# A layer kernel on one core: full-height content matmuls, PSUM tiles emptied by two engines, and a content copy moved behind the exponentials

## The reference

```
xn = layernorm(x)
c_q = xn @ Wq_down          # latent 64
c_kv = xn @ Wkv_down        # latent 64
q_c = c_q @ Wq_up;  k_c = c_kv @ Wk_up;  v_c = c_kv @ Wv_up      # 128 heads x 4
q_r = xn @ Wq_rope          # 128 heads x 64
k_r = xn @ Wk_rope          # 64, shared by all heads
scores = (q_c . k_c + q_r . k_r) / sqrt(68)
s = (softmax(scores) @ v_c) @ Wo
g = silu(ffn(xn))
out = x + s * g
```

## Time and profile before

| | |
|---|---|
| median of the runs | 2092.19 us |
| the profiled execution's own time | 2091.22 us |
| its span | 2089.4 us |
| TensorE busy | 2027.3 us (97%) |
| VectorE, ScalarE, GpSimd busy | 1396.4, 1068.5, 496.7 us |
| preamble, up to the first matmul of attention | 104.36 us |

### The profile page before, as it was taken

The page is one execution under the profiler, slowest core; times in us unless marked ns, Lnnn a source line. Parts: engine busy times, 40 slices in busy tenths (PEclk is TensorE's granted clock), DMA queues, the critical chain, the costliest instruction groups (busy, mean ns, idle before and its releaser), DMA issues. The chain is left out here.

```text
span 2089.4 us, 38976 instructions
## 1 busy us (share of the span) xinstructions
PE 2027.3 (97%) x12576; PEld 1542.7 (74%) x12576; DVE 1396.4 (67%) x1606; ACT 1068.5 (51%) x1549; POOL 496.7 (24%) x771
## 2 busy tenths in 40 slices
PE   6989999999999999999999999999999999978998
PEld 4567777777777777777777777777777777746776
DVE  5376676666766676667666766676667666736764
ACT  3635555555555555555555555555555555542222
POOL 2122222222213232223132212231322222133221
PEclk7989999999999999999999999999999999999999
DMA  5511212121212121212121111111111111131221
GB/s 181 189 32 34 44 29 47 27 48 28 47 28 48 25 46 27 48 28 47 28 45 30 41 32 40 36 37 38 38 36 36 37 37 30 26 110 64 88 85 45
DMA packets 128841, 102.70 MB, mean 49 GB/s; under 512 B 51494, under 2 KB 94502, under 8 KB 128798
## 3 DMA queue, kind: packets, MB, share of 16 engines
q1 hardware_dynamic: 128798, 102.15, 20.9%
HBM read 50.71 MB, written 25.17 MB: 36 GB/s over the span
## 5 line engine op out<-in xcount | busy, mean ns | idle before, releaser
L707 DVE TENSOR_REDUCE mx<-sx 128x4 f32<-128x1024 f32 x512 | 627.1, 1225 | 501.3 <-PE sx L789 483.1
L687 ACT ACTIVATE probs<-st 128x1024 f32<-128x1024 f32 x512 | 512.0, 1025 | 150.3 <-PE st L772 148.7
L657 ACT ACTIVATE slot<-pj 64x512 fp32r<-64x512 f32 x512 | 303.9, 594 | 485.2 <-PE pj L802 478.9
L606 POOL CAST k<-kc 64x512 fp32r<-64x512 f32 x256 | 167.3, 654 | 1199.0 <-PE st L772 1198.7
L772 PE MATMUL st<-slot,k 89*128 89x512 f32 x1024 | 423.7, 414 | 10.3 <-ACT probs L687 2.8
L802 PE MATMUL pj<-xh,wh 128*128 128x512 f32 x1024 | 402.7, 393 | 4.6 <-PEq L154 3.6
L772 PE MATMUL st<-slot,krlh 128*128 128x512 f32 x1024 | 406.8, 397 | 0.0
L802 PE MATMUL pj<-xh,wl 128*128 128x512 f32 x1024 | 402.1, 393 | 0.0
L802 PE MATMUL pj<-xl,wh 128*128 128x512 f32 x1024 | 401.8, 392 | 0.0
L717 DVE TENSOR_TENSOR slot<-pj,slot 64x512 fp32r<-64x512 f32 x512 | 352.7, 689 | 16.3 <-ACT slot L657 0.3
L789 PEld LDWEIGHTS sx<-k,slot 88*128 88x128 f32 x2048 | 307.0, 190 | 65.6 <-issue 27.2
(11 more groups left out here) (172 smaller groups left out, 1406.4 us busy)
## 6 DMA issues: line engine op xcount, KB each, us to landing
w_stage<-in_Wq_rope SPq DMA_DIRECT2D x64, 256.0 KB, 3.1
c_scratch<-stage SPq DMA_DIRECT2D x32, 256.0 KB, 2.5
c_in<-c_scratch SPq DMA_DIRECT2D x128, 64.0 KB, 1.9
o_scratch<-o_sb SPq DMA_DIRECT2D x128, 64.0 KB, 2.2
k<-kc SPq DMA_DIRECT2D x128, 48.0 KB
slot<-kc SPq DMA_DIRECT2D x256, 24.0 KB
k<-kx SPq DMA_DIRECT2D x128, 48.0 KB
slot<-kx SPq DMA_DIRECT2D x256, 24.0 KB
```

What stands on the lines that cost most here:

```text
L606: nc.gpsimd.tensor_copy(k1[0:64, s, :, :].rearrange("p a n -> p (a n)"), krh[:, bp * CH:(bp + 1) * CH]).then_inc(k_ready, 1)
L657: nc.scalar.activation(slot1[0:64, (k - 1) % NS, e, :, :], pj[64 * e:64 * e + 64, :].rearrange("p (a n) -> p a n", a=2), ACT.Copy).then_in ...
L687: nc.scalar.activation(probs[:, k % NS, kt], st[:, kt], ACT.Exp, scale=SCALE).then_inc(exp_done, 1)
L707: nc.vector.tensor_reduce(mx[:, p, lo:lo + 4], sx[:, :, :].rearrange("p a (b k) -> p (a b) k", b=2), axis=AX.X, op=ALU.max).then_inc(red_d ...
```

## The change

It has five parts.

1. The low-part content matmuls (L413, L417, L421) take all 128 rows of `upl` and `cs` and not 64 of them. They then also add low x low, which is tiny.
2. Of the 12 content tiles of chunks 0 to 2, ScalarE empties ten and VectorE two (n = 3 and 8); of chunk 3, every second one goes to VectorE. One semaphore for each engine's tiles takes the place of the common one.
3. On VectorE `normalise` of the next chunk comes after the two remainders of `cs`, and not ahead of them behind the statistics. The remainders `xl` are spread between its tiles, and the statistics of the chunk after next stand at the end.
4. `project` multiplies by `wsh` first and by `wsl` last, and only the `wsl` matmuls wait for GpSimd. GpSimd's `wsl` waits for the first chunk's `xn`. Transposes stand ahead of odd tiles. The first content block `kc` is made behind chunk 1 and not at the end.
5. In attention `content_hi` comes behind the three exponentials of its step.

The diff, cut to its core:

```diff
+        def by_vector(u):
+            return u % NE % 2 == 1 if u // NE == NC - 1 else u % NE in (3, 8)
+        def wait_tile(eng, u):
+            done = sum(by_vector(v) == by_vector(u) for v in range(u + 1))
+            eng.wait_ge(dve_tiles if by_vector(u) else act_tiles, done)
...
             pool.wait_ge(ws_hi, 1)
+            pool.wait_ge(xn_ready, NTL)
             nc.gpsimd.tensor_tensor(wsl[:, :, :], ws[:, :, :], wsh[:, :, :], ALU.subtract).then_inc(ws_ready, 1)
...
                 for n in range(NE):
-                    if n % 2 == 0 and n < 2 * NTL and c + 1 < NC:
+                    u = c * NE + n
+                    if n % 2 == 1 and n < 2 * NTL and c + 1 < NC:
                         hi_transposed(c + 1, n // 2)
-                    u = c * NE + n
-                    act.wait_ge(ev_done, u + 1)
-                    if u >= NST:
-                        act.wait_ge(stored[u % NST], 16 * (u // NST))
-                    nc.scalar.activation(stage[:, u % NST, :], ev[n % 4][:, :], ACT.Copy).then_inc(st_ready, 1)
+                    if not by_vector(u):
+                        act.wait_ge(ev_done, u + 1)
+                        if u >= NST:
+                            act.wait_ge(stored[u % NST], 16 * (u // NST))
+                        nc.scalar.activation(stage[:, u % NST, :], ev[n % 4][:, :], ACT.Copy).then_inc(act_tiles, 1)
...
                 if c + 2 < NC:
                     root(c + 2)
-            act.wait_ge(c_loaded, 32)
-            nc.scalar.activation(kc[64:128, 0:CH], c_in[64:128, :], ACT.Copy).then_inc(ct_hi, 1)
+                if c == 1:
+                    act.wait_ge(c_loaded, 32)
+                    nc.scalar.activation(kc[64:128, 0:CH], c_in[64:128, :], ACT.Copy).then_inc(ct_hi, 1)
...
                 nc.vector.tensor_tensor(cs[0:64, 1, :], cp[64:128, :], cs[64:128, 1, :], ALU.subtract).then_inc(c_lo, 1)
+                if c + 1 < NC:
+                    normalise(c + 1)
                 dve.wait_ge(krh_done, 2 * c + 2)
                 nc.vector.tensor_tensor(krlh[0:64, xs], kp[0:64, :], krh[:, xs], ALU.subtract).then_inc(krl_done, 1)
-                if c + 1 < NC:
-                    for i in range(NTL):
-                        lo_transposed(c + 1, i)
+                for n in range(NE):
+                    u = c * NE + n
+                    if n % 2 == 1 and n < 2 * NTL and c + 1 < NC:
+                        lo_transposed(c + 1, n // 2)
+                    if by_vector(u):
+                        dve.wait_ge(ev_done, u + 1)
+                        if u >= NST:
+                            dve.wait_ge(stored[u % NST], 16 * (u // NST))
+                        nc.vector.tensor_copy(stage[:, u % NST, :], ev[n % 4][:, :]).then_inc(dve_tiles, 1)
                 if c + 2 < NC:
                     statistics(c + 2)
-                    normalise(c + 2)
...
                 for k in range(KD):
-                    for n, (w, xx) in enumerate(((wsh, xh), (wsh, xl), (wsl, xh))):
...
+                    for n, xx in enumerate((xh, xl)):
+                        nc.tensor.matmul(dst[:, :], wsh[:, k, lo:lo + 128], xx[:, k, xs],
+                                         start=(k == 0 and n == 0), stop=False)
+                pe.wait_ge(ws_ready, 1)
+                for k in range(KD):
+                    last = nc.tensor.matmul(dst[:, :], wsl[:, k, lo:lo + 128], xh[:, k, xs],
+                                            start=False, stop=(k == KD - 1))
...
-                    nc.tensor.matmul(ev[n % 4][:, :], upl[0:64, 0, i], cs[0:64, 0, :],
+                    nc.tensor.matmul(ev[n % 4][:, :], upl[:, a, i], cs[:, a, :],
                                      start=False, stop=True).then_inc(ev_done, 1)
...
-                if s == 2 and k < STEPS and at.live(k + 2):
-                    content_hi(k // NS + 1, at.turn(k) + 1)
...
                 if k % 2 == 0 and at.live(k - 3) and k - 3 < STEPS:
                     exponentials(at, k - 3, 0)
+                if s == 2 and k < STEPS and at.live(k + 2):
+                    content_hi(k // NS + 1, at.turn(k) + 1)
```

More of the change, by code:

```diff
@@ L195, in project_inputs @@
         ev_done = sem("ev_done")
-        st_ready = sem("st_ready")
+        act_tiles = sem("act_tiles")
+        dve_tiles = sem("dve_tiles")
+        def by_vector(u):
[3 more added lines that the diff above has]
+            eng.wait_ge(dve_tiles if by_vector(u) else act_tiles, done)
         def by_launch(t, a, j):
@@ L225, in _ @@
                 for n in range(NE):
-                    sp.wait_ge(st_ready, c * NE + n + 1)
+                    wait_tile(sp, c * NE + n)
                     i = n % NTL
@@ L382, in _ @@
             statistics(1)
-            normalise(1)
             for c in range(NC):
                 chunk(c)
-            dve.wait_ge(ct_hi, 1)
-            nc.vector.tensor_tensor(kc[64:128, 2 * CH:3 * CH], c_in[64:128, :], kc[64:128, 0:CH],
-                                    ALU.subtract).then_inc(ct_lo, 1)
+                if c == 1:
+                    dve.wait_ge(ct_hi, 1)
+                    nc.vector.tensor_tensor(kc[64:128, 2 * CH:3 * CH], c_in[64:128, :], kc[64:128, 0:CH],
+                                            ALU.subtract).then_inc(ct_lo, 1)
         @block.tensor
@@ L400, in project @@
             def project(c, dst, lo, done):
+                xs = slice(c * CH, (c + 1) * CH)
                 for k in range(KD):
-                    for n, (w, xx) in enumerate(((wsh, xh), (wsh, xl), (wsl, xh))):
-                        last = nc.tensor.matmul(dst[:, :], w[:, k, lo:lo + 128], xx[:, k, c * CH:(c + 1) * CH],
-                                                start=(k == 0 and n == 0), stop=(k == KD - 1 and n == 2))
+                    for n, xx in enumerate((xh, xl)):
[5 more added lines that the diff above has]
+                                            start=False, stop=(k == KD - 1))
                 last.then_inc(done, 1)
@@ L409, in raise_up @@
                 u = c * NE + n
-                wait(pe, st_ready, u - 3)
-                if a == 0:
-                    nc.tensor.matmul(ev[n % 4][:, :], uph[:, 0, i], cs[:, 0, :], start=True, stop=False)
-                    nc.tensor.matmul(ev[n % 4][:, :], upl[0:64, 0, i], cs[0:64, 0, :],
[L414 to L417, removed]
+                if u >= 4:
+                    wait_tile(pe, u - 4)
+                if a < 2:
+                    nc.tensor.matmul(ev[n % 4][:, :], uph[:, a, i], cs[:, a, :], start=True, stop=False)
+                    nc.tensor.matmul(ev[n % 4][:, :], upl[:, a, i], cs[:, a, :],
                                      start=False, stop=True).then_inc(ev_done, 1)
@@ L420, in raise_up @@
                     nc.tensor.matmul(ev[n % 4][:, :], cs[:, 1, i], uph[:, 2, :], start=True, stop=False)
-                    nc.tensor.matmul(ev[n % 4][:, :], cs[64:128, 1, i], upl[64:128, 2, :],
+                    nc.tensor.matmul(ev[n % 4][:, :], cs[:, 1, i], upl[:, 2, :],
                                      start=False, stop=True).then_inc(ev_done, 1)
@@ L428, in _ @@
                 pe.wait_ge(xl_done, (c + 1) * NTL)
-                if c == 0:
-                    pe.wait_ge(ws_ready, 1)
+                pe.wait_ge(ws_hi, 1)
                 wait(pe, c_lo, 2 * c)
```

## The result

The changed kernel takes 2041.03 us (median of four runs, 2040.73 to 2042.02) against 2092.16 us: a ratio of 0.9756, 95% interval 0.9739 to 0.9773. The forecast was 2043.7 us. The profiled execution took 2042.02 us with a span of 2040.2, so 49.2 us of span are gone. By milestones: attention starts at 76.53 and not at 104.36 us (27.8 us), attention itself is 22.2 us shorter (from its first matmul to the last group of `ob`, 1742.2 before and 1720.0 after), and what follows is 0.8 us longer.

The account below looks back on a forecast made before the run. TensorE, busy for 97% of the span, bounds it, slowed by weight-load stalls, low clock and waits. 2091.22 less 26.8 (preamble) and 21.7 (attention) gives 2042.7; the median lies 1.0 above, so 2043.7, range 2035 to 2058.

Parts of the forecast that it names:

- content behind the exponentials: Attention: 62 steps go from 6.94 to 6.59 us with the content copy after the third exponential, 21.7 us.
- Start: Chunk 0's start: wsl waits for normalise, so the first projection starts at 15.1 and not 16.9; bounds 0 to 2.1 us.
- The hold: Before the first content stage: content begins at 23.3, 5.1 us earlier, and idle time and low clock nearly go.
- Content stages: Chunks 0 to 2: chunk 0 takes 10.0 us; later chunks 14.2, of which content 8.6, with ScalarE late.
- the step that I had priced at 0 to 0.5: VectorE's statistics and ScalarE's root before the next cs, with kc in chunk 1: hidden, 0.5 us if not.
- The stall: Content pairs: 0.24 us idle ahead of 64-row weight loads goes with 128 rows; two matmuls then 0.23 us apart.
- Rival 1: Preamble: 64 rows cost nothing, content stays at 11.8 us a chunk; gain 15.6 and not 26.8, 2055; chance 0.06.
- Rival 2: Clock stays low in chunk 0 as TensorE waits: 5 us, 2049; through the whole preamble 2073; chance 0.09.
- Chunk 3: Last content stage: six stage buffers and stores at 0.84 us each hold it; twelfth tile written by 76.7.
- End of the preamble: Last tile to attention: kc made earlier, leaving 0.35 of DMA issue and 0.5; attention starts at 77.6.
- Rival 3: Attention: exponentials' own wait takes over, moving the copy gives little; half the gain 2055, none 2065; chance 0.10.
- Rival 4: Attention: GpSimd's copies hold VectorE's content remainder past its 0.9 us to spare; 2087 to 2130; chance 0.03.

Follow-up runs that it names:

- e4: Changed kernel with VectorE's normalise of the next chunk back behind the statistics, ahead of the remainders of cs; 2050.52 us.
- e6: Changed kernel with ScalarE emptying all content tiles, none left to VectorE; 2040.57 us.
- e2: Kernel before with one edit, low-part content matmuls on 128 rows; 2072.73 us.
- e1: Changed kernel with the low-part content matmuls on 64 rows again; 2054.20 us.
- e5: Kernel before, low parts still on 64 rows, content tiles taken two at a time (high, high, low, low); 2081.04 us.
- e10: Changed kernel with eight stage buffers and not six; 2041.23 us.
- e7: Changed kernel with the first content block made at the end of the preamble again; 2040.40 us.
- e11: Kernel before with attention's content copy behind the exponentials and nothing else; 2070.34 us.
- e3: Changed kernel with attention's content copy ahead of the exponentials again; 2065.40 us.

## Why the prediction was right, step by step

The direction, the time (2.7 us off) and both halves of the sum held: 26.8 forecast and 27.8 measured for the preamble, 21.7 and 22.2 for attention (0.8 more behind it). The three large terms (no stall between rows, no hold, content behind the exponentials) came about as described. That the preamble came out within 1.1 us owes something to luck: against the forecast the start was 1.0 us late, the stretch to the first content matmul 0.7 short, chunk 0's stage 1.4 short, chunk 1 0.8 short, chunk 2 1.3 long, and the rest 0.5 short.

*Start.* The first projection was forecast for 15.1 and came at 16.13, because in this execution VectorE waited 1.25 us for x. From the first `normalise` to the first projection it took 6.63 us and not 8.24: 1.6 us of the 1.8.

*The hold.* Forecast 23.3 for the first content matmul, measured 23.63, 7.50 us behind the first projection where 8.2 had been forecast; TensorE didn't wait at all. The low clock went with the hold. e4 puts the hold back and shows both: the waits and the clock.

*Content stages.* 10.0 forecast for chunk 0, 8.6 measured; 14.2 for each later chunk, 13.4 and 15.5 measured. The mean was right and the reason not: the stage isn't ScalarE's. With all tiles on ScalarE chunks 1 and 2 take 0.3 and 0.2 us more (e6), and in the order before a stage with all of them takes 7.39 us (e2). What is late is VectorE: chunk 2's `cs` waits 0.7 us for it, the step that I had priced at 0 to 0.5, and its `xl` 1.4 us, which I had counted for chunk 0 alone.

*The stall.* The prediction read the idle time as standing ahead of the 64-row loads alone. It stands ahead of the 128-row load behind a 64-row matmul too (0.24 us in e1), so there are two stalls in a pair; the sum didn't suffer, since it took the distances between starts from both.

*Rival 1* (rows cost nothing) fell with e1; its price, 2055, is what e1 measured (2054.2). The trace and the Trainium skill's TensorEngine Tiling (Array Packing), section Tiling Modes, agree here: changing the mode drains the engine. e5 shows it apart from the row count.

*Rival 2* (the clock stays low because TensorE waits for tiles and for `xl`) did not come about in the changed kernel, whose third transposes waited 1.08 us in chunk 0 at a granted clock of 1.00. It was close: in e6's execution the same wait was 2.00 us, and the clock fell.

*Chunk 3.* I had given the stores 0.84 us each from the mean of a stretch that wasn't full; they go at 0.68. That term was mis-sized: the last tile was forecast for 76.7 and came at 75.55, of which 0.6 us come from chunk 3's earlier start. e10 shows that the stores do limit this stage, and that it is the rate of the queues and not the number of buffers.

*End of the preamble.* 1.0 us measured, 0.9 forecast. But the edit is not worth the 2.0 us credited to it, since it gives 1.0 back in chunk 2 (e7).

*Content behind the exponentials.* The step went from 6.94 to 6.58, forecast 6.59. e11 shows the gain without the rest of the change, e3 the loss. Rival 3 fell. Rival 4 did not come about: VectorE gets the high part first, by 0.13 us, and its remainder takes its plain 0.69, as all 63 of them do (689 to 691 ns). Whether GpSimd first would hold it wasn't tried.

Open: what makes up the 1960.5 to 1966.3 us of attention and tail among kernels that are alike there. Both parts move: up to the last `ob` matmul attention takes 1719.4 to 1723.3 us in these ten, and behind it the fourteen profiled kernels take 240.8 to 243.6, with the same code. The 0.8 us behind attention lie inside that and are no loss that can be told.

## What to carry to other kernels

Look at the idle time of weight loads: a "full" TensorE with starts 0.42 us apart, where others lie 0.23 apart, was not full, and making the smaller matmul larger took the stall away. Where a step in one turn is longer than the same step in a turn without one copy, the difference is that copy's price, whatever the totals say. Ask of a run that meets its forecast where the time lies: e6 had the forecast figure from another stage. Behind the largest term look for what limits the new pace as a rate (here the store queues): more buffers don't move it.

## What the runs showed of the hardware that I had not expected

In the first content stage, counted from its first content matmul, the clock stayed at its low level for 19.58 us with a switch at each matmul and for 16.02 with a switch at every second, and rose within 9.41 us without switches, though TensorE's busy time was the same as the stretch's length in all three. At the high level the same stalls (e1, 11.7 us a stage) never brought it down. So the stalls cost twice: 0.2 us each at full clock, and the clock where a stage starts cold.

A wait inside the content stage left the granted clock at 1.00 where it was 1.08 or 1.39 us long (changed kernel), and was followed by the low level where it was 2.00 (e6); the holds of 1.89 to 4.40 us ahead of the stages in e4 all had a part at the low level behind them. These are single cases, and no rule follows from them.

A DMA issue on SyncE took 0.33 us with room in the queues and up to 0.65 us when they were full, so a full queue shows on the issuing engine.

`normalise` of four tiles, SBUF to SBUF, took 3.35 us beside one cast and two subtractions of GpSimd, 4.32 where two casts and two subtractions ran beside nearly all of it (e6), and 1.92 without them, while GpSimd's cast took 0.81 and not 0.61 us beside it. VectorE's tile copies out of PSUM took 0.67 to 0.69 us in either case. The Trainium skill's SBUF — State Buffer, section SBUF: two separate sides, says that VectorE, in a two-port mode or with two SBUF inputs, and GpSimd lock a shared pair of ports against each other for a whole instruction; the times agree in direction.
